# Softmax row sums counted by fours: every second pair sum is added to its neighbour by an accumulating DMA from GpSimd's queue

## Chip, cores and metric

One core of a Trainium2 chip. The metric is the device time of one execution in microseconds (us), the median over several runs; the comparison after the change is made in the same way.

## The reference

Input x is 16 samples of 192 channels by 32x32 positions (N = 1024 tokens), float32. The block is a group norm over 32 groups of 6 channels, six-head self-attention (head size 32), an output projection with a bias, and the residual.

```
...
        B, C, H, W = x.shape
        N = H * W
        xt = x.reshape(B, C, N).transpose(0, 2, 1)
        qkv = jnp.einsum('bnc,oc->bno', xt, qkv_w)
        qkv = qkv.reshape(B, N, 3, NUM_HEAD, DIM_HEAD).transpose(2, 0, 3, 1, 4)
        q, k, v = (qkv[0], qkv[1], qkv[2])
        attn = jnp.einsum('bhnd,bhmd->bhnm', q, k) * SCALE
        attn = jax.nn.softmax(attn, axis=-1)
        out = jnp.einsum('bhnm,bhmd->bhnd', attn, v)
        out = out.transpose(0, 2, 1, 3).reshape(B, N, C)
        out = jnp.einsum('bnc,oc->bno', out, proj_w) + proj_b
...
    x = x + _L0_conv_ref(_gn(x), L0_conv_qkv_w, L0_conv_proj_w, L0_conv_proj_b)
```

## The kernel before

The program is written as one instruction stream per engine, with semaphores between them. Work is cut into **steps**, one per sample (16 with attention, and a few at either end), and each step into 24 **slots**: three pairs of heads times eight tiles of 128 keys. In slot s TensorE makes the transposed scores of one key tile against all 1024 queries for the two heads of the pair, as four matmuls of 512 queries (units u = 0 to 3, `score`, L528). ScalarE turns each into exponentials `probs` (L681). TensorE then multiplies `probs` by V (`weigh`, L543), and needs their sum over the keys for the softmax's denominator.

**The denominator.** GpSimd adds the `probs` of slots s-1 and s elementwise (L751, two instructions, one for each head `a`), at the odd slots, into a ring of four `prob_pairs`. TensorE multiplies such a pair sum by a matrix of ones (`count`, L558), which adds up its 128 keys, and accumulates the four pairs of a head pair in the bank `sums_ps`. Then, once per head pair: ScalarE copies the sums (`copy_sums`, L656), SP spreads them over 128 partitions (L386), VectorE inverts them (L887), SP gathers and broadcasts them through DRAM (L393, L396), GpSimd divides the heads by them (L725), ScalarE and GpSimd split the result in two float16 parts (L624, L730), and SP moves these to the projection's operands (L411).

**Around it, in the same slots.** `row_max` (L453) makes the scores of twelve slots ahead for VectorE's row maxima (L825). `fill` (L511 to L516) makes, at fixed slots, one piece of the next sample's Q, K and V or of the last sample's projection. ScalarE and VectorE split the new Q and K in two float16 parts, `qk_hi` (L601) and `qk_lo` (L868), in one buffer. The last of the six pieces is made at slot 6; then, from slot 7 on, SP copies them within on-chip memory to the stacked operands `q_stack` and `k_stack` (`stack_pair`, L358), six DMAs of 128 KB for each head pair, at slots 7, 9 and 11. At slot 10 SP also loads the next x, 1 MB in three DMAs (L344, L346). At slot 13 ScalarE takes the first Q and K piece of the sample after the next into the same `qk_hi`, and so waits first until all 18 copies have landed:

```
                    if i == 0 and due(st.b + 2):

                        for p in range(PAIRS):
                            act.wait_ge(stacked[p], MOVE * STACK_MOVES * (st.b + 2))
```

ScalarE's queue is in order: the exponentials of slot 13 stand behind this wait, and TensorE has two score banks. What stands in which slot is given by tables (`QK_LATE_SLOTS`, `STACK_SLOTS`, `LOAD_SLOT`, `SUMS_TAKEN` and its neighbours), and `due(s, offset, every)` says which unit of work is due `offset` slots after it began. GpSimd issues no DMA in this kernel.

Of the kernel before, what the change touches and what calls it, by code (L numbers as in the profile page):

```python
# [16 lines left out]
C = 192  # L17
# [61 lines left out]
PAIR = 2  # L79
PAIR_COUNTED = PAIR + 3  # L80
PAIRS_A_HEAD = TILES // PAIR

HEADS_TAKEN = TILES
SUMS_TAKEN = TILES + 4
SUMS_SPREAD = TILES + 5
INVERTED = TILES + 6
INV_SPREAD = TILES + 7
DIVIDED = TILES + 11
MOVED = (23, 22, 22)
# [108 lines left out]
def group_norm_attention(nc, x, qkv_wT, proj_wT, proj_b, group_mean, identity, out):  # L198


    with ExitStack() as ctx:
        def sb(name, shape, dt):
            return ctx.enter_context(nc.sbuf_tensor(name, shape, dt))
# [18 lines left out]
        probs = sb("probs", [P, 2, RING, N], F32)  # L222
        prob_pairs = sb("prob_pairs", [P, 2, PAIR_RING, N], F32)

# [24 lines left out]

        w_f32 = prob_pairs[:, 0, 0:2, 0:3 * C]  # L250
        wp_f32 = prob_pairs[:, 0, 2:4, 0:C]
        w_abs = prob_pairs[:, 1, 0:2, 0:3 * C]
        wp_abs = prob_pairs[:, 1, 2:4, 0:C]
        w_hi = sb("w_hi", [P, 2, 3 * C], F16)
# [175 lines left out]
        def _(pe):  # L430
# [118 lines left out]
            def count(b, q):  # L549

                p, at_pair = divmod(q, PAIRS_A_HEAD)
                pe.wait_ge(pairs_added, 2 * (SLOTS // PAIR * b + q + 1))
                if at_pair == 0 and due(PAIRS * b + p):
                    pe.wait_ge(sums_taken, PAIRS * b + p)
                for half in range(HALVES):
                    for a in range(2):
                        at = D * (2 * half + a)
                        last = pe.matmul(sums_ps[at:at + D, :], ones[:, 0:D],  # L558
                                         prob_pairs[:, a, q % PAIR_RING, HALF * half:HALF * (half + 1)],
                                         start=(at_pair == 0), stop=(at_pair == PAIRS_A_HEAD - 1))  # L560
                last.then_inc(sums_done, 1)
# [5 lines left out]
            def step(st):  # L567
                for s in range(SLOTS):
                    for u in range(SCORE_UNITS):
# [18 lines left out]
        def _(act):  # L588
# [60 lines left out]
            def copy_sums(st, s):  # L649

                for j, par, p in st.due(s, SUMS_TAKEN, TILES):
                    k = PAIRS * j + p
                    act.wait_ge(sums_done, PAIRS_A_HEAD * (k + 1))
                    if due(k):
                        act.wait_ge(sums_spread_out, MOVE * k)
                    nc.scalar.copy(sums_sb[:, :], sums_ps[:, :]).then_inc(sums_taken, 1)  # L656
# [35 lines left out]
        def _(pool):  # L692
            nc.gpsimd.memset(k_stack[STACK:SHIFTED, :, :, :], SHIFT).then_inc(shift_set, 1)

            def step(st):
                for s in range(SLOTS):
                    if st.project_in and s == VAR_SLOT:

# [43 lines left out]
                    if st.attend and s % 2 == 1:  # L742

                        j = s // 2
                        for a in range(2):
                            pool.wait_ge(probs_ready, SCORE_UNITS * (SLOTS * st.b + s) + 2 * (a + 1))
                            counted = SLOTS // PAIR * st.b + j - PAIR_RING + 1
                            if a == 0 and due(counted):

                                pool.wait_ge(sums_done, counted)  # L750
                            nc.gpsimd.tensor_tensor(prob_pairs[:, a, j % PAIR_RING, :],  # L751
                                                    probs[:, a, (s - 1) % RING, :],
# [178 lines left out]
```

## Time and profile before

| | |
|---|---|
| median of 3 runs | 1878.63 us (1876.38 to 1881.58) |
| the profiled execution | 1886.8 us, span 1885.0 us |
| TensorE's mean granted clock | 0.96 |
| busy, TensorE / VectorE / ScalarE / GpSimd | 92% / 61% / 67% / 63% |
| moved by DMA | 109.28 MB, mean 58 GB/s |

The span is the time from the first to the last instruction; the profiled execution's own time is 1.8 us more. Busy shares are means over the whole span, and a matmul's row overlaps the next one's, so how much an instruction costs TensorE is read from the starts of the rows around it. The DMA share is the mean busy share of the core's 16 DMA engines.

### The profile page before, as it was taken

To read this page: it belongs to the slowest core of one execution; us is meant where nothing else is said; L and a number is where in the kernel's file an instruction comes from. 1 tells how busy PE (TensorE), PEld (TensorE's weight loads), DVE (VectorE), ACT (ScalarE), POOL (GpSimd) and SP (SyncE) were. 2 spreads that over 40 slices of the span, in tenths; PEclk is the share of its full clock that TensorE was granted. 3 is DMA by queue.
4 is the path that set the end of the run, shared out by engine and by line. 5 is a ranking of instruction groups with operands and counts; after the bars stand their busy time and mean duration, and the time that the engine had idled before them with its cause. 6 is when DMAs were issued, how large, how long until landed. Compare 5 with 4: busy or idle time off the path is not lost.

```text
span 1885.0 us, 30321 instructions
## 1 busy us (share of the span) xinstructions
PE 1727.9 (92%) x9440; PEld 531.2 (28%) x9440; DVE 1156.5 (61%) x2022; ACT 1257.5 (67%) x2033; POOL 1182.0 (63%) x613
## 2 busy tenths in 40 slices
PE   3799999999998999999999999999989999999993
PEld 1233223323232232322323222332223223222220
DVE  2577767666666666656666656766656666666710
ACT  1247777866677676766868667786666768777781
POOL 3126767755676666666766666675567666767783
PEclk9989999998999999999999999999999999999995
DMA  2404141402414033151402314141151404132102
GB/s 67 73 1 79 30 89 41 91 20 58 86 46 85 27 74 56 48 94 49 80 18 75 67 47 85 41 88 26 53 91 46 85 20 90 23 78 43 58 19 73
DMA packets 74285, 109.28 MB, mean 58 GB/s; under 512 B 26176, under 2 KB 39040, under 8 KB 74112
## 3 DMA queue, kind: packets, MB, share of 16 engines
q1 hardware_dynamic: 74112, 107.13, 26.8%
q8 instruction: 89, 1.46, 0.3%
q14 instruction: 84, 0.69, 0.1%
HBM read 42.99 MB, written 12.98 MB: 30 GB/s over the span
## 4 chain that ended last, share of the span: by engine, by line
PE 71%; DMA 10%; SPq 8%; ACT 4%; issue 4%; DVE 2%; POOL 1%; ACTq 0%; POOLq 0%; DVEq 0%
PE max_ps L453 17%; PE heads_ps L543 16%; PE scores_ps L528 15%; PE sums_ps L558 9%; DMA k_stack<-qk_lo 8%; SPq L358 6%; ACT probs L681 3%; PE extra_ps L516 2%; PE extra_ps L511 2%; PE extra_ps L512 2%; PE extra_ps L513 2%; PE extra_ps L515 2%; DMA inv_rows<-inv_spread 1%; PE extra_ps L475 1%; PE extra_ps L474 1%
## 5 line engine op out<-in xcount | busy, mean ns | idle before, releaser
L825 DVE TENSOR_REDUCE half_max<-max_ps 128x1 f32<-128x512 f32 x1536 | 1012.1, 685 | 524.7 <-PE max_ps L453 489.2
L681 ACT ACTIVATE probs<-scores_ps,exp_scale 128x512 f32<-128x512 f32 x1536 | 995.4, 686 | 442.0 <-PE scores_ps L528 416.7
L751 POOL TENSOR_TENSOR prob_pairs<-probs 128x1024 f32<-128x1024 f32 x384 | 898.2, 2357 | 482.2 <-ACT probs L681 480.0
L528 PE MATMUL scores_ps<-q_stack,k_stack 98*128 98x512 f16 x1536 | 598.5, 391 | 77.5 <-ACT probs L681 61.4
L453 PE MATMUL max_ps<-k_stack,q_stack 96*128 96x512 f16 x1536 | 608.1, 398 | 4.2 <-DMA k_stack<-qk_lo 2.2
L543 PE MATMUL heads_ps<-probs,v_sb 128*32 128x512 f32 x3072 | 416.4, 615 | 0.0
L453 PEld LDWEIGHTS max_ps<-k_stack,q_stack 96*128 96x128 f16 x1536 | 150.5, 98 | 615.6 <-issue 514.9
L558 PE MATMUL sums_ps<-prob_pairs,ones 128*32 128x512 f32 x1536 | 215.3, 634 | 1.7 <-POOL prob_pairs L751 1.7
L528 PEld LDWEIGHTS scores_ps<-q_stack,k_stack 98*128 98x128 f16 x1536 | 151.8, 99 | 219.4 <-ACT probs L681 132.3
L740 POOL TENSOR_TENSOR x_res<-projected,x_res 96x512 f32<-96x512 f32 x64 | 81.1, 1267 | 82.3 <-ACT projected L613 82.3
L868 DVE TENSOR_TENSOR qk_lo<-extra_ps,qk_hi 128x512 f16<-128x512 f32 x96 | 66.0, 688 | 86.9 <-ACT qk_hi L601 84.7
L601 ACT CAST qk_hi<-extra_ps 128x512 f16<-128x512 f32 x96 | 55.8, 581 | 91.2 <-DMA k_stack<-qk_lo 53.7
L543 PEld LDWEIGHTS heads_ps<-probs,v_sb 128*32 128x32 f32 x3072 | 61.1, 109 | 157.4 <-issue 147.1
L636 ACT ACTIVATE xhat<-x_sb,neg_mu_rstd,rstd 128x512 f32<-128x512 f32 x64 | 51.2, 806 | 40.1 <-POOL neg_mu_rstd L703 40.1
L725 POOL TENSOR_TENSOR heads_out<-heads_sb,inv_sb 128x512 f32<-128x512 f32 x48 | 60.7, 1265 | 17.1 <-DMA inv_sb<-inv_rows 15.1
L700 POOL TENSOR_TENSOR rstd<-var_eps,minus_half 128x2 f32<-128x2 f32 x16 | 11.2, 701 | 92.1 <-DVE var_eps L862 92.1
L730 POOL TENSOR_TENSOR heads_lo<-heads_out,heads_hi 128x512 f16<-128x512 f32 x48 | 55.4, 1154 | 14.0 <-ACT heads_hi L624 14.0
L613 ACT ACTIVATE projected<-extra_ps,bias,proj_unscale 96x512 f32<-96x512 f32 x64 | 49.4, 772 | 15.6 <-PE extra_ps L516 15.6
L511 PE MATMUL extra_ps<-xhat_a_hi,w_hi 128*128 128x512 f16 x96 | 38.5, 401 | 17.2 <-POOL xhat_b L716 9.4
L558 PEld LDWEIGHTS sums_ps<-prob_pairs,ones 128*32 128x32 f32 x1536 | 30.8, 109 | 68.4 <-issue 61.5
L511 PE MATMUL extra_ps<-attn_a_hi,wp_hi 128*96 128x512 f16 x64 | 25.4, 397 | 23.7 <-DMA attn_b<-heads_lo 21.1
L802 DVE BATCH_NORM_STATS2 half_stats<-x_sb 128x6 f32<-128x512 f32 x64 | 43.2, 682 | 0.0
(92 smaller groups left out, 1018.4 us busy)
## 6 DMA issues: line engine op xcount, KB each, us to landing
q_stack<-qk_hi SPq DMA_DIRECT2D x96, 128.0 KB, 4.4
k_stack<-qk_hi SPq DMA_DIRECT2D x96, 128.0 KB, 5.6
inv_sb<-inv_rows SPq DMA_DIRECT2D x48, 256.0 KB
x_res<-x SPq DMA_DIRECT2D x16, 768.0 KB, 5.4
out<-x_res SPq DMA_DIRECT2D x16, 768.0 KB, 4.8
x_sb<-x SPq DMA_DIRECT2D x16, 512.0 KB, 7.3
x_sb<-x SPq DMA_DIRECT2D x32, 256.0 KB, 8.7
q_stack<-qk_lo SPq DMA_DIRECT2D x48, 128.0 KB, 4.2
```

What stands on the lines that cost most here:

```text
L358: sp.dma_start(stack[D * n:D * (n + 1), par, 2 * p:2 * p + 2, :], part[row % P:row % P + 2 * D, row // P, :]).then_inc(stacked[p], MOVE)
L453: pe.matmul(max_ps[:, bank, :], q_stack[0:STACK, par, h, P * tile:P * (tile + 1)], k_stack[0:STACK, par, h, HALF * half:HALF * (half + 1)] ...
L511: pe.matmul(to, hi[:, 0, :], a_hi, start=True, stop=False)
L528: pe.matmul(scores_ps[:, u_bank(s, u), :], k_stack[0:SHIFTED, st.parity, h, P * tile:P * (tile + 1)], q_stack[0:SHIFTED, st.parity, h, HAL ...
L543: last = pe.matmul(heads_ps[at:at + D, :], v_sb[:, par, tile, D * h:D * (h + 1)], probs[:, a, s % RING, HALF * half:HALF * (half + 1)], st ...
L558: last = pe.matmul(sums_ps[at:at + D, :], ones[:, 0:D], prob_pairs[:, a, q % PAIR_RING, HALF * half:HALF * (half + 1)], start=(at_pair == ...
L681: nc.scalar.activation(probs[:, a, s % RING, HALF * half:HALF * (half + 1)], scores_ps[:, u_bank(s, u), :], ACT.Exp, scale=exp_scale[:, 0: ...
L725: nc.gpsimd.tensor_tensor(heads_out[:, :], heads_sb[:, (par + p) % 2, :], inv_sb[:, :], ALU.mult).then_inc(divided, 1)
L740: nc.gpsimd.tensor_tensor(x_res[:, t, n], projected[:, i % 2, :], x_res[:, t, n], ALU.add).then_inc(residual_added, 1)
L751: nc.gpsimd.tensor_tensor(prob_pairs[:, a, j % PAIR_RING, :], probs[:, a, (s - 1) % RING, :], probs[:, a, s % RING, :], ALU.add).then_inc( ...
L825: nc.vector.tensor_reduce(half_max[:, a, tile, half:half + 1], max_ps[:, bank, :], AX_X, ALU.max).then_inc(max_read[bank], 1)
L868: nc.vector.tensor_tensor(qk_lo[:, t, n], extra_ps[:, :], qk_hi[:, t, n], ALU.subtract).then_inc(extra_freed, 1)
```

## The change

GpSimd's pair sums stay. When both pairs of a quad (four slots) are there, GpSimd issues a DMA with an adding operation, from `prob_pairs` of the even pair onto that of the odd pair: 128 partitions of 8 KB, both heads at once, for which the tensor's axes are swapped so that the two heads of a ring place lie side by side. TensorE counts only the summed place, once in four slots instead of twice. The wait of `count` is on the DMA's semaphore. The count of a quad is due eight slots after its first tile (a pair's was five), so the sums, their inverse and the division each come one slot later; `MOVED`, the slots of L411, stays. In a ring place's reuse, the even one waits for the DMA that reads it, the odd one for the count. There are 96 such DMAs in all, six in a step.

```
@@ -77,15 +77,17 @@
 PAIR = 2
-PAIR_COUNTED = PAIR + 3
-PAIRS_A_HEAD = TILES // PAIR
+QUAD = 4
+QUAD_ADDED = QUAD
+QUAD_COUNTED = QUAD + 4
+QUADS_A_HEAD = TILES // QUAD
...
-SUMS_TAKEN = TILES + 4
...
-DIVIDED = TILES + 11
+SUMS_TAKEN = TILES + 5
...
+DIVIDED = TILES + 12
...
@@ -548,16 +552,16 @@
             def count(b, q):
 
-                p, at_pair = divmod(q, PAIRS_A_HEAD)
-                pe.wait_ge(pairs_added, 2 * (SLOTS // PAIR * b + q + 1))
+                p, at_quad = divmod(q, QUADS_A_HEAD)
+                pe.wait_ge(quad_summed[at_quad], MOVE * (PAIRS * b + p + 1))
...
-                                         prob_pairs[:, a, q % PAIR_RING, HALF * half:HALF * (half + 1)],
...
+                                         prob_pairs[:, (2 * q + 1) % PAIR_RING, a, HALF * half:HALF * (half + 1)],
...
@@ -692,8 +696,18 @@
+            def sum_quad(b, q):
+
+                pool.wait_ge(pairs_added, 4 * (SLOTS // QUAD * b + q + 1))
+                pool.sem_inc(quad_begun, 1)
+                pool.dma_start(prob_pairs[:, (2 * q + 1) % PAIR_RING, :, :].rearrange("p a n -> p (a n)"),
+                               prob_pairs[:, 2 * q % PAIR_RING, :, :].rearrange("p a n -> p (a n)"),
+                               accum_op=ALU.add).then_inc(quad_summed[q % QUADS_A_HEAD], MOVE)
+
             def step(st):
                 for s in range(SLOTS):
+                    for j, par, q in st.due(s, QUAD_ADDED, QUAD):
+                        sum_quad(j, q)
...
-                            counted = SLOTS // PAIR * st.b + j - PAIR_RING + 1
-                            if a == 0 and due(counted):
-
-                                pool.wait_ge(sums_done, counted)
-                            nc.gpsimd.tensor_tensor(prob_pairs[:, a, j % PAIR_RING, :],
+                            q, second = divmod(j - PAIR_RING, 2)
+                            if a == 0 and second == 0 and due(PAIRS * st.b + q // 2 + 1):
+
+                                pool.wait_ge(quad_summed[q % 2], MOVE * (PAIRS * st.b + q // 2 + 1))
+                            elif a == 0 and second == 1 and due(SLOTS // QUAD * st.b + q + 1):
+
+                                pool.wait_ge(sums_done, SLOTS // QUAD * st.b + q + 1)
+                            nc.gpsimd.tensor_tensor(prob_pairs[:, j % PAIR_RING, a, :],
                                                     probs[:, a, (s - 1) % RING, :],
                                                     probs[:, a, s % RING, :], ALU.add).then_inc(pairs_added, 1)
```

Where the instructions stand now. GpSimd's queue, slots 7 to 11 of a step in the loop (the first L751 row is the second half of slot 7's pair, the next two are slot 9's pair, L707 and L716 make low parts of the normalised x; register rows are left out), before:

```order
L751 TENSOR_TENSOR prob_pairs<-probs 128x1024 [waits probs_ready]
...
L707 TENSOR_TENSOR xhat_a_lo<-xhat,xhat_a_hi 128x1024 [waits xhat_ready]
...
L751 TENSOR_TENSOR prob_pairs<-probs 128x1024 [waits sums_done]
...
L751 TENSOR_TENSOR prob_pairs<-probs 128x1024 [waits probs_ready]
...
L716 TENSOR_TENSOR xhat_b<-xhat,xhat_b 64x1024 [waits pairs_added]
...
L725 TENSOR_TENSOR heads_out<-heads_sb,inv_sb 128x512 [waits heads_lo_ready,inv_broadcast]
```

and with the change (line numbers are those of the changed file: L768 is the pair sum, L703 the adding DMA):

```order
L768 TENSOR_TENSOR prob_pairs<-probs 128x1024 [waits probs_ready]
...
L703 DMA prob_pairs<-prob_pairs 128x2048 [waits pairs_added]
...
L721 TENSOR_TENSOR xhat_a_lo<-xhat,xhat_a_hi 128x1024 [waits xhat_ready]
...
L768 TENSOR_TENSOR prob_pairs<-probs 128x1024 [waits quad_summed0]
...
L768 TENSOR_TENSOR prob_pairs<-probs 128x1024 [waits probs_ready]
...
L730 TENSOR_TENSOR xhat_b<-xhat,xhat_b 64x1024 [waits pairs_added]
...
L768 TENSOR_TENSOR prob_pairs<-probs 128x1024 [waits sums_done,probs_ready]
...
L768 TENSOR_TENSOR prob_pairs<-probs 128x1024 [waits probs_ready]
...
L703 DMA prob_pairs<-prob_pairs 128x2048 [waits pairs_added]
...
L739 TENSOR_TENSOR heads_out<-heads_sb,inv_sb 128x512 [waits heads_lo_ready,inv_broadcast]
```

Two adding DMAs, of the quads of slots 4 to 7 and 8 to 11, now stand behind the pairs of slots 7 and 11, and the division has moved behind the second of them.

SP's queue, slots 5 to 7 of a step (L380 are shift rows for the scores, L411 the moved heads, L358 the first stack), before:

```order
L386 DMA sums_spread<-sums_sb 128x1x16 [waits sums_taken]
L380 DMA q_stack<-shift_rows 1x16x128 [waits shift_step]
L380 DMA q_stack<-shift_rows 1x16x128
L411 DMA attn_a_hi<-heads_hi 64x512 [waits heads_lo_ready]
L411 DMA attn_a_lo<-heads_lo 64x512
L411 DMA attn_a_hi<-heads_hi 64x512
L411 DMA attn_a_lo<-heads_lo 64x512
L358 DMA q_stack<-qk_hi 32x2x1024 [waits extra_freed]
L358 DMA q_stack<-qk_lo 32x2x1024
```

and now:

```order
L384 DMA q_stack<-shift_rows 1x16x128 [waits shift_step]
L384 DMA q_stack<-shift_rows 1x16x128
L390 DMA sums_spread<-sums_sb 128x1x16 [waits sums_taken]
L415 DMA attn_a_hi<-heads_hi 64x512 [waits heads_lo_ready]
L415 DMA attn_a_lo<-heads_lo 64x512
L415 DMA attn_a_hi<-heads_hi 64x512
L415 DMA attn_a_lo<-heads_lo 64x512
L362 DMA q_stack<-qk_hi 32x2x1024 [waits extra_freed]
L362 DMA q_stack<-qk_lo 32x2x1024
```

The spreading of the sums has moved behind the shift rows; the order of L411 and L358 (now L415, L362) is the same, but the `heads_lo` that L415 waits for is made one slot later on GpSimd.

TensorE's queue at an odd slot with a count before (L558, here followed by a row maximum and a score):

```order
L516 MATMUL extra_ps<-xhat_b,w_lo 128x512
L552 ISA
L558 MATMUL sums_ps<-prob_pairs,ones 32x512 [waits pairs_added]
L558 MATMUL sums_ps<-prob_pairs,ones 32x512 x3
L453 MATMUL max_ps<-k_stack,q_stack 128x512 [waits max_read1]
L527 ISA
L528 MATMUL scores_ps<-q_stack,k_stack 128x512 [waits probs_ready]
```

and at one of the slots, a multiple of four, where a count stands now (L562):

```order
L519 MATMUL extra_ps<-xhat_b,w_hi 128x512
L520 MATMUL extra_ps<-xhat_b,w_lo 128x512
L562 MATMUL sums_ps<-prob_pairs,ones 32x512 [waits quad_summed1]
L562 MATMUL sums_ps<-prob_pairs,ones 32x512 x3
L457 MATMUL max_ps<-k_stack,q_stack 128x512 [waits max_read1]
L532 MATMUL scores_ps<-q_stack,k_stack 128x512 [waits probs_ready]
```

The group is the same four matmuls; its wait has gone from GpSimd's pair to the DMA's semaphore, and there are half as many groups.

## Rows read from the trace of the kernel before

**Rows 1.** The page's head: busy us, share of the span, instructions.

```profile
PE 1727.9 (92%) x9440; PEld 531.2 (28%) x9440; DVE 1156.5 (61%) x2022; ACT 1257.5 (67%) x2033; POOL 1182.0 (63%) x613
```

**Rows 2.** The page's chain that ended last, share of the span by engine.

```profile
PE 71%; DMA 10%; SPq 8%; ACT 4%; issue 4%; DVE 2%; POOL 1%; ACTq 0%; POOLq 0%; DVEq 0%
```

**Rows 3.** The page's group of the counting matmuls, eight instructions for each count.

```profile
L558 PE MATMUL sums_ps<-prob_pairs,ones 128*32 128x512 f32 x1536 | 215.3, 634 | 1.7 <-POOL prob_pairs L751 1.7
```

**Rows 4.** Timeline around a count: start, duration (us), engine, line, tiles.

```profile
910.72 0.38 PE L453 MATMUL max_ps<-k_stack,q_stack 96*128 96x512 f16 x1
...
910.94 0.38 PE L528 MATMUL scores_ps<-q_stack,k_stack 98*128 98x512 f16 x1
...
911.25 1.06 PE L558 MATMUL sums_ps<-prob_pairs,ones 128*32 128x512 f32 x8
...
912.24 0.39 PE L453 MATMUL max_ps<-k_stack,q_stack 96*128 96x512 f16 x1
```

**Rows 5.** What L601 waits for (us, times); first and last such wait in the timeline.

```profile
  DMA k_stack<-qk_lo: 53.7, 12
...
272.97 0.58 ACT L601 CAST qk_hi<-extra_ps 128x512 f16<-128x512 f32 x1 [3.53 <-DMA k_stack<-qk_lo]
...
1504.21 0.58 ACT L601 CAST qk_hi<-extra_ps 128x512 f16<-128x512 f32 x1 [4.54 <-DMA k_stack<-qk_lo]
```

**Rows 6.** Timeline at one of these waits (idle before it in brackets).

```profile
831.77 0.58 ACT L601 CAST qk_hi<-extra_ps 128x512 f16<-128x512 f32 x1 [4.72 <-DMA k_stack<-qk_lo]
...
834.61 1.93 PE L558 MATMUL sums_ps<-prob_pairs,ones 128*32 128x512 f32 x8
```

**Rows 7.** SP's queue in that step: moved heads, first copies, last copy, store.

```profile
799.44 0.59 SPq L411 DMA_DIRECT2D attn_a_hi<-heads_hi  x1
...
802.88 0.60 SPq L358 DMA_DIRECT2D q_stack<-qk_hi  x1
...
810.65 0.56 SPq L358 DMA_DIRECT2D q_stack<-qk_hi  x1
...
819.73 0.60 SPq L358 DMA_DIRECT2D k_stack<-qk_lo  x1
...
882.53 0.52 SPq L423 DMA_DIRECT2D out<-x_res  x1
```

**Rows 8.** Stretches: five engines' busy us, granted clock, DMA share, GB/s.

```profile
808.00:811.00 3.00, 3.00 (x22) 1.47 (x24) 2.09 (x4) 2.60 (x5) 2.13 (x2) 1.00 0.14 25
...
811.00:814.00 3.00, 3.00 (x21) 0.58 (x14) 1.87 (x3) 2.99 (x6) 2.06 (x1) 1.00 0.74 152
814.00:820.00 6.00, 5.88 (x35) 1.67 (x33) 4.27 (x7) 4.44 (x8) 5.61 (x4) 1.00 1.07 163
...
826.00:829.00 3.00, 2.68 (x15) 0.65 (x14) 1.05 (x2) 1.05 (x2) 0.16 (x1) 1.00 0.78 103
...
883.00:886.00 3.00, 1.69 (x11) 0.35 (x10) 0.05 (x1) 0.90 (x2) 0.31 (x1) 1.00 0.91 281
```

**Rows 9.** The same stretch of two steps, with and without a load of x.

```profile
811.00:828.00 17.00, 16.88 (x103) 4.73 (x95) 10.66 (x17) 12.51 (x21) 13.84 (x7) 1.00 1.00 158
...
1596.00:1613.00 17.00, 16.88 (x99) 5.01 (x98) 11.43 (x19) 12.57 (x21) 13.99 (x8) 1.00 0.57 86
```

**Rows 10.** GpSimd's timeline in that step.

```profile
791.16 1.16 POOL L730 TENSOR_TENSOR heads_lo<-heads_out,heads_hi 128x512 f16<-128x512 f32 x1
795.04 4.67 POOL L751 TENSOR_TENSOR prob_pairs<-probs 128x1024 f32<-128x1024 f32 x2 [2.72 <-ACT probs L681]
803.37 4.67 POOL L751 TENSOR_TENSOR prob_pairs<-probs 128x1024 f32<-128x1024 f32 x2 [3.65 <-ACT probs L681]
...
820.37 4.68 POOL L751 TENSOR_TENSOR prob_pairs<-probs 128x1024 f32<-128x1024 f32 x2
```

**Rows 11.** The last count and what TensorE waits for behind it.

```profile
1843.25 1.06 PE L558 MATMUL sums_ps<-prob_pairs,ones 128*32 128x512 f32 x8 [1.66 <-POOL prob_pairs L751]
...
1865.41 0.63 PE L511 MATMUL extra_ps<-attn_a_hi,wp_hi 128*96 128x512 f16 x1 [21.10 <-DMA attn_b<-heads_lo]
```

More of the change, by code:

```diff
@@ L79 @@
 PAIR = 2
-PAIR_COUNTED = PAIR + 3
-PAIRS_A_HEAD = TILES // PAIR
+QUAD = 4
+QUAD_ADDED = QUAD
+QUAD_COUNTED = QUAD + 4
+QUADS_A_HEAD = TILES // QUAD
 HEADS_TAKEN = TILES
-SUMS_TAKEN = TILES + 4
-SUMS_SPREAD = TILES + 5
-INVERTED = TILES + 6
-INV_SPREAD = TILES + 7
-DIVIDED = TILES + 11
+SUMS_TAKEN = TILES + 5
+SUMS_SPREAD = TILES + 6
+INVERTED = TILES + 7
+INV_SPREAD = TILES + 8
+DIVIDED = TILES + 12
 MOVED = (23, 22, 22)
@@ L222, in group_norm_attention @@
         probs = sb("probs", [P, 2, RING, N], F32)
-        prob_pairs = sb("prob_pairs", [P, 2, PAIR_RING, N], F32)
+        prob_pairs = sb("prob_pairs", [P, PAIR_RING, 2, N], F32)
         xhat_a_hi = sb("xhat_a_hi", [P, 2, N], F16)
@@ L247, in group_norm_attention @@
         projected = sb("projected", [OM, 2, HALF], F32)
[L250 to L253, printed above, removed]
+        w_f32 = prob_pairs[:, 0:2, 0, 0:3 * C]
+        wp_f32 = prob_pairs[:, 2:4, 0, 0:C]
+        w_abs = prob_pairs[:, 0:2, 1, 0:3 * C]
+        wp_abs = prob_pairs[:, 2:4, 1, 0:C]
         w_hi = sb("w_hi", [P, 2, 3 * C], F16)
@@ L305, in group_norm_attention @@
         pairs_added = sem("pairs_added")
+        quad_begun = sem("quad_begun")
+        quad_summed = [sem(f"quad_summed{i}") for i in range(QUADS_A_HEAD)]
         heads_done = sem("heads_done")
@@ L549, in count @@
             def count(b, q):
-                p, at_pair = divmod(q, PAIRS_A_HEAD)
-                pe.wait_ge(pairs_added, 2 * (SLOTS // PAIR * b + q + 1))
-                if at_pair == 0 and due(PAIRS * b + p):
+                p, at_quad = divmod(q, QUADS_A_HEAD)
+                pe.wait_ge(quad_summed[at_quad], MOVE * (PAIRS * b + p + 1))
+                if at_quad == 0 and due(PAIRS * b + p):
                     pe.wait_ge(sums_taken, PAIRS * b + p)
@@ L558, in count @@
                         last = pe.matmul(sums_ps[at:at + D, :], ones[:, 0:D],
-                                         prob_pairs[:, a, q % PAIR_RING, HALF * half:HALF * (half + 1)],
-                                         start=(at_pair == 0), stop=(at_pair == PAIRS_A_HEAD - 1))
+                                         prob_pairs[:, (2 * q + 1) % PAIR_RING, a, HALF * half:HALF * (half + 1)],
+                                         start=(at_quad == 0), stop=(at_quad == QUADS_A_HEAD - 1))
                 last.then_inc(sums_done, 1)
@@ L579, in step @@
                         if u == COUNT_UNIT:
-                            for j, par, q in st.due(s, PAIR_COUNTED, PAIR):
+                            for j, par, q in st.due(s, QUAD_COUNTED, QUAD):
                                 count(j, q)
@@ L652, in copy_sums @@
                     k = PAIRS * j + p
-                    act.wait_ge(sums_done, PAIRS_A_HEAD * (k + 1))
+                    act.wait_ge(sums_done, QUADS_A_HEAD * (k + 1))
                     if due(k):
```

## Prediction

> **What bounds the kernel now.** I read the page's head first: TensorE is busy 92% of the span, ScalarE 67%, GpSimd 63% [rows 1]. That looks as if TensorE work taken out came off the time one for one. The chain that ended last says otherwise: only 71% of the span lies on TensorE, 10% on DMA transfers and 8% on SP's queue [rows 2]. So a part of every step is bound by something that TensorE doesn't do. To find it I asked who ends ScalarE's idle time at L601: the copies to `k_stack`, 53.7 us in 12 waits, some 4.5 us each, one in each of 12 consecutive steps, from 272.97 to 1504.21 us, which is 11 periods of 111.9 us [rows 5]. In one of them, at 831.77 us, ScalarE has stood 4.72 us; the exponentials stand behind it, so TensorE stands too, and its next count takes 1.93 us, where one takes 1.06 elsewhere [rows 4, 6].
>
> Why are the copies late? SP begins them at 802.88 and issues the last at 819.73 [rows 7], and it lands only when ScalarE goes on, 12 us later. The DMA share is 0.14 at 808 to 811 us, 0.74 at 811 to 814, and 1.07 at 814 to 820 [rows 8]; over 811 to 828 us it is 1.00 [rows 9]. The engines are full: copies and the load of x queue up behind each other. The step without a load of x is a natural experiment. In the like stretch its share is 0.57, TensorE runs through (16.88 busy of 17), and it isn't among the 12 waits [rows 5, 9]. One plain transfer of 1 MB more or less in this window makes or unmakes the wait.
>
> So a step has two parts. From slot 7 (the last `qk_lo` piece) to slot 13 (ScalarE goes on) the length is set by SP's issues and the DMA engines, about 29 us (802.88 to 831.77). In the other 18 slots it is TensorE's order that sets it.
>
> **What is removed.** 96 of 192 counts. From a score to the next instruction TensorE needs 0.22 us; with a count between it is 1.30 (910.94 to 912.24) [rows 4]. So 1.08 us each, 104 us in all; the group's busy time, half of 215.3 us [rows 3], says the same. A step gives 6.5 us. But of its 12 counts three stand in slots 7 to 12, where the end is set by a landing, and what is saved there only makes ScalarE wait sooner. Outside stand nine, at odd slots; with the change four, at slots 16, 20, 0 and 4. That is 5 x 1.08 = 5.4 us a step that counts.
>
> **What is added.** Six adding DMAs a step, each 128 rows of 8 KB. The trace has no such DMA, nor any from GpSimd, so I bound it. Let E be the time for which one fills all 16 engines. The stretch with the 768 KB store of the output (issued 882.53) moves 281 GB/s at share 0.91 [rows 7, 8], so 309 GB/s at full share: 1.05 MB take 3.4 us. That is the low end, a copy in long rows beside little else. An adding DMA must read the destination as well as the source, so twice that, 6.8 us, is the value that I take. The load of x, also 1 MB, costs (1.00 - 0.57) x 17 = 7.3 us of engine time beside the copies [rows 9]. Reading twice at that price gives the high end, about 15.
>
> The Trainium skill, "Collectives: The Full Stack", section "The bandwidth ceiling: the fold count and why AG ≠ RS ≠ AR", says the same of reductions in a DMA engine: they are half as fast as copies because each chunk needs two source reads on one ring, not because the add costs time. By that rule E is twice the copy, whatever the copy costs. No run here shows it yet.
>
> **Where the six lie.** GpSimd issues a quad's DMA behind its second pair. Two matter. The pair of slot 7 ends at 803.37 + 4.67 = 808.04, that of slot 11 at 820.37 + 4.68 = 825.05 [rows 10]. The issue itself is unseen: between SP's 0.6 us [rows 7] and one pair sum's 2.3 us [rows 10]; I take 1.2. GpSimd is idle 37% of the span [rows 1] and waits for probs before each pair, which hides it. So the DMAs start near 809.3 and 826.3.
>
> The first meets 1.5 us of idle engines until 811 (0.86 of 1.7 us) and 0.8 until 814 (0.26 of 3); the rest, E - 2.3, pushes the whole backlog back. The second starts when, with that push, copies for several microseconds are still queued (826 to 829 shows 0.78 even before the change [rows 8]); nearly all of it goes before the last copy, E - 0.8. A third thing is late: `heads_lo` of the second head pair was ready at 791.16 + 1.16 and is now made behind the pair that ends at 795.04 + 4.67 = 799.7, so at 800.9. SP waits for it before the first copy: its four issues took from 799.44 to about 802, and now go from 800.9 to 803.5, so the copies start 0.6 us later [rows 7, 10].
>
> The landing that ScalarE waits for moves by 0.6 + (E - 2.3) + (E - 0.8) = 2E - 2.5. With E = 6.8 that is 11.1 us, its wait grows to 16 to 18 us, and a step changes by 11.1 - 5.4 = +5.7. Twelve steps: +68 us.
>
> **The rest.** The first step and the last with a copy have spare share (0.57) and I set them at zero. Two more steps have no such copies and gain 6.5 each: -13. At the end, the last count stood right behind the last pair (1843.25), and 21 us later TensorE still waits for what follows from it [rows 11]; now the DMA stands between, 1.2 for the issue and 6.8 for the transfer: +8. The other quads find idle engines, and TensorE counts four slots (some 17 us) after their issue, so they cost nothing while E plus latency is under that; if this cover goes, TensorE and all behind it waits. The swapped axes cost nothing: the pair sum still reads and writes 1024 contiguous elements. The later inverse and division hide behind the same 24-slot order; what is late next is the SP issue counted above.
>
> Sum: 68 - 13 + 8 = +63 us, against the profiled execution 1886.8 to 1950. That execution is 8 us above the median, so I give 1878.6 + 63 = **1942 us**. In general: 1878.6 + 12 (2E - 7.9) - 5.
>
> **Rivals.**
> - *The adding DMA is cheap* (E near 3.4: the reads overlap). A step changes by -1.1, the total is 1860. It turns at 2E - 7.9 = 0.4, so E = 4.15 us. For it: 309 GB/s is what these engines reach in long rows [rows 8]. Against: the x load, in rows of 4 KB, cost 7.3 us in this very window. Chance 0.17.
> - *The copies aren't pushed* (the engines give SP's queue its turns, and the gain outside arrives in full): 1878.6 - 12 x 5.4 - 13 + 8 = 1809. Against it: the x load alone made the wait. Chance 0.07.
> - *The adding DMA is slow* (E of 10 to 15). At E = 12 the step grows by 16.1, 2067; at 15 it is 2139. Then the first quad, beside the copies, also comes too late for the count of slot 12, which adds TensorE's wait to ScalarE's. For it: copies here run at 163 GB/s at share 1.07, half of the store's rate [rows 8]. Chance 0.16.
> - *Forecast*, E between 5 and 9: 1900 to 1996. Chance 0.60.
>
> In sentences of their own: the Trainium skill, "DMA: Bandwidth & Descriptors", section "Anatomy of one DMA — SWDGE (gpsimd) path", gives a fit, 2.0 us fixed plus bytes over 436 GB/s. By it, as an estimate, 1 MB fills the engines 2.4 us, and the total would be about 1836, by the first rival's mechanism. The trace's copies (163 GB/s) disagree with the rate, the store (281) comes closer; for an adding DMA no row here decides.
>
> **How the numbers follow.** 1942 is the likeliest case's value at E = 6.8. The range must leave out at most 2 in 10: 1855 takes in nearly all of the cheap case, 2067 the slow one up to E = 12. About 0.3% (6 us) is what a measurement of this kernel can tell from none. Faster by more: the cheap case but a slice near its turn, and the unpushed case, 0.22. Within: that slice, 0.05. Slower: 0.73.
>
> **What would show each step.** In the changed profile: the counting group at x768 and half the busy time; L605 (L601 now) waiting for `k_stack` 12 or more times with 12 to 20 us each, where it was 4.5; a period of about 118 us; the DMA share at 1.0 from some 809 us of the step's like place through the wait, and in the 20-to-4 slots between 0.2 and 0.5; the adding DMA's 16 engines filled for 6.8 us. Wrong: an E under 4.15, waits at L605 that stay under 10 us, or waits of TensorE at L562 for the DMA of 5 us and more in each step, which would say that the DMA's own latency, not its share of the engines, decides.

## The result, and the profile after

The changed kernel takes 1954.45 us (median of 4 runs, 1949.09 to 1960.23), the kernel before, run beside it, 1877.51 (1872.37 to 1881.58). The ratio is 1.0406, with a 95% interval of 1.0378 to 1.0434: slower by 77 us. The forecast was 1942.

The page of the changed kernel's profile (line 1: busy time and share of each engine; the queue lines: packets, MB, share of the 16 engines over the span; then the chain that ended last, then groups of instructions, then a DMA group):

```profile
span 1958.4 us, 28917 instructions
PE 1666.9 (85%) x8672; PEld 523.6 (27%) x8672; DVE 1154.4 (59%) x2022; ACT 1245.4 (64%) x2033; POOL 1270.0 (65%) x709
...
q0 software_dynamic: 13824, 100.67, 26.2%
q1 hardware_dynamic: 74112, 107.13, 25.2%
...
PE 45%; DMA 15%; SPq 13%; POOL 12%; issue 7%; ACT 4%; DVE 2%; POOLq 0%; ACTq 0%; DVEq 0%
...
L605 ACT CAST qk_hi<-extra_ps 128x512 f16<-128x512 f32 x96 | 56.5, 589 | 226.7 <-DMA k_stack<-qk_lo 189.2
...
L703 POOL DMA_DIRECT2D prob_pairs<-prob_pairs x96 | 84.7, 882 | 56.9 <-POOL prob_pairs L768 55.5
L562 PE MATMUL sums_ps<-prob_pairs,ones 128*32 128x512 f32 x768 | 106.6, 628 | 11.3 <-DMA prob_pairs<-prob_pairs 11.3
...
prob_pairs<-prob_pairs POOLq DMA_DIRECT2D x96, 1024.0 KB, 8.5
```

The counting group is half of what it was [rows 3]. The chain on TensorE went from 71% [rows 2] to 45%. ScalarE's wait for `k_stack` took 53.7 us [rows 5] and takes 189.2. GpSimd's queue q0 is the adding DMAs alone: 26.2% of 1958.4 us over 96 is **E = 5.34 us** each, and one lands 8.5 us after its issue (median). The DMA is almost never waited for by its own reader: TensorE lost 11.3 us to it in all, at one place, the last count.

One step, that of [rows 6 to 10]. First ScalarE, on the timeline (start, duration, in brackets the idle time before it and what ended it):

```profile
864.93 0.59 ACT L605 CAST qk_hi<-extra_ps 128x512 f16<-128x512 f32 x1 [15.15 <-DMA k_stack<-qk_lo]
```

then SP's queue:

```profile
828.20 0.60 SPq L362 DMA_DIRECT2D q_stack<-qk_hi  x1
...
836.34 1.28 SPq L362 DMA_DIRECT2D q_stack<-qk_hi  x1
837.66 1.39 SPq L362 DMA_DIRECT2D q_stack<-qk_lo  x1
...
844.18 0.61 SPq L362 DMA_DIRECT2D q_stack<-qk_hi  x1
...
847.41 0.59 SPq L362 DMA_DIRECT2D k_stack<-qk_lo  x1
```

GpSimd's two issues in the window:

```profile
828.36 4.67 POOL L768 TENSOR_TENSOR prob_pairs<-probs 128x1024 f32<-128x1024 f32 x2 [2.73 <-ACT probs L685]
833.61 0.87 POOL L703 DMA_DIRECT2D prob_pairs<-prob_pairs  x1 [0.59 <-POOL prob_pairs L768]
...
849.18 0.88 POOL L703 DMA_DIRECT2D prob_pairs<-prob_pairs  x1 [0.58 <-POOL prob_pairs L768]
```

and stretches of the same step (length, busy us of PE, PEld, DVE, ACT, POOL with counts, granted clock, DMA share, GB/s):

```profile
828.00:834.00 6.00, 6.00 (x43) 2.67 (x45) 4.49 (x8) 5.53 (x11) 5.06 (x3) 1.00 0.62 143
834.00:842.00 8.00, 7.75 (x44) 1.81 (x36) 5.35 (x9) 6.84 (x13) 7.76 (x5) 1.00 0.95 186
842.00:850.00 8.00, 8.00 (x52) 2.76 (x52) 5.25 (x9) 5.46 (x9) 7.18 (x5) 1.00 1.06 175
850.00:859.00 9.00, 2.88 (x21) 0.56 (x13) 0.69 (x1) 0.00 (x0) 1.36 (x2) 0.80 1.09 193
859.00:865.00 6.00, 0.00 (x0) 0.00 (x0) 0.00 (x0) 0.07 (x1) 0.00 (x0) 0.50 0.33 78
865.00:872.00 7.00, 5.84 (x18) 1.49 (x19) 4.43 (x9) 5.18 (x9) 5.23 (x3) 0.50 0.01 1
872.00:880.00 8.00, 7.87 (x45) 2.70 (x44) 6.13 (x11) 5.52 (x10) 4.52 (x3) 0.97 0.15 36
```

Read together: the first adding DMA is issued at 833.61, and the share goes to 0.95 and stays near or over 1.0 until 859. From 850 to 859 TensorE is busy only 2.88 us, and from 859 until ScalarE goes on nothing computes. The copies' first issue to ScalarE's going on takes 828.20 to 864.93, 36.7 us, where it was 28.9 [rows 6, 7]. SP's own issues, 0.60 us each before, take up to 1.39 in the microseconds behind the first adding DMA's issue; at 844.18, with the share at 1.06, they take 0.61 again. TensorE's granted clock falls to 0.50 (the lower level, 1.2 GHz) while it stands, stays there until 872 although it works again from 865 on, and is back at 0.97 in the stretch from 872.

Twelve waits of about 15 us (14.74 at 280.60, 15.18 at 1564.76) stand in the place of the twelve of 4.5; two shorter ones, 3.64 at 171.37 and 5.95 at 1670.38, are new. The period is (1564.76 - 280.60)/11 = 116.7 us, where it was 111.9 [rows 5].

The end of the program, on the timeline:

```profile
1914.67 1.94 PE L562 MATMUL sums_ps<-prob_pairs,ones 128*32 128x512 f32 x8 [11.28 <-DMA prob_pairs<-prob_pairs]
```

The last pair sum ended at 1901.03 + 4.91 = 1905.94 on GpSimd; the last count, once right behind it, now stands 8.7 us later.

**Where the 73.4 us of the span went** (1885.0 to 1958.4). Up to the first of the twelve waits +7.6 (272.97 to 280.60), in the eleven periods after it +52.9, from the last wait to the end of the last pair sum +2.2, and behind it +10.7.

### The profile page after: what moved, and what is told of

Same layout as the page of the kernel before. It is cut to its first block, busy times and chain, and to the rows that moved or that the text cites. A ratio compares the mean times of both kernels' runs of the same rounds, so it can differ in the third digit from the quotient of the medians.

```text
span 1958.4 us, 28917 instructions
## 1 busy us (share of the span) xinstructions
PE 1666.9 (85%) x8672; PEld 523.6 (27%) x8672; DVE 1154.4 (59%) x2022; ACT 1245.4 (64%) x2033; POOL 1270.0 (65%) x709
## 3 DMA queue, kind: packets, MB, share of 16 engines
q0 software_dynamic: 13824, 100.67, 26.2%
q1 hardware_dynamic: 74112, 107.13, 25.2%
## 4 chain that ended last, share of the span: by engine, by line
PE 45%; DMA 15%; SPq 13%; POOL 12%; issue 7%; ACT 4%; DVE 2%; POOLq 0%; ACTq 0%; DVEq 0%
DMA k_stack<-qk_lo 12%; PE max_ps L457 11%; PE scores_ps L532 11%; PE heads_ps L547 11%; SPq L362 10%; POOL prob_pairs L768 9%; ACT probs L685 3%; PE sums_ps L562 3%; DMA inv_rows<-inv_spread 2%; SPq L415 2%; PE extra_ps L520 2%; POOL heads_out L739 1%; PE extra_ps L515 1%; PE extra_ps L516 1%; PE extra_ps L519 1%
## 5 line engine op out<-in xcount | busy, mean ns | idle before, releaser
L768 POOL TENSOR_TENSOR prob_pairs<-probs 128x1024 f32<-128x1024 f32 x384 | 898.1, 2358 | 473.7 <-ACT probs L685 469.7
L532 PE MATMUL scores_ps<-q_stack,k_stack 98*128 98x512 f16 x1536 | 609.9, 398 | 200.3 <-ACT probs L685 169.2
L547 PE MATMUL heads_ps<-probs,v_sb 128*32 128x512 f32 x3072 | 423.9, 625 | 0.9 <-ACT probs L685 0.9
L605 ACT CAST qk_hi<-extra_ps 128x512 f16<-128x512 f32 x96 | 56.5, 589 | 226.7 <-DMA k_stack<-qk_lo 189.2
L703 POOL DMA_DIRECT2D prob_pairs<-prob_pairs x96 | 84.7, 882 | 56.9 <-POOL prob_pairs L768 55.5
L562 PE MATMUL sums_ps<-prob_pairs,ones 128*32 128x512 f32 x768 | 106.6, 628 | 11.3 <-DMA prob_pairs<-prob_pairs 11.3
L754 POOL TENSOR_TENSOR x_res<-projected,x_res 96x512 f32<-96x512 f32 x64 | 85.5, 1336 | 40.5 <-ACT projected L617 40.5
L739 POOL TENSOR_TENSOR heads_out<-heads_sb,inv_sb 128x512 f32<-128x512 f32 x48 | 74.9, 1560 | 20.4 <-DMA inv_sb<-inv_rows 20.4
L628 ACT CAST heads_hi<-heads_out 128x512 f16<-128x512 f32 x48 | 29.7, 619 | 29.3 <-POOL heads_out L739 29.3
L904 DVE RECIPROCAL inv_spread<-sums_spread 128x16 f32<-128x16 f32 x48 | 11.7, 244 | 61.8 <-DMA sums_spread<-sums_sb 61.8
## 6 DMA issues: line engine op xcount, KB each, us to landing
x_res<-x SPq DMA_DIRECT2D x16, 768.0 KB, 10.7
```

The source lines that it names most:

```text
L532: pe.matmul(scores_ps[:, u_bank(s, u), :], k_stack[0:SHIFTED, st.parity, h, P * tile:P * (tile + 1)], q_stack[0:SHIFTED, st.parity, h, HAL ...
L547: last = pe.matmul(heads_ps[at:at + D, :], v_sb[:, par, tile, D * h:D * (h + 1)], probs[:, a, s % RING, HALF * half:HALF * (half + 1)], st ...
L562: last = pe.matmul(sums_ps[at:at + D, :], ones[:, 0:D], prob_pairs[:, (2 * q + 1) % PAIR_RING, a, HALF * half:HALF * (half + 1)], start=(a ...
L703: pool.dma_start(prob_pairs[:, (2 * q + 1) % PAIR_RING, :, :].rearrange("p a n -> p (a n)"), prob_pairs[:, 2 * q % PAIR_RING, :, :].rearra ...
L739: nc.gpsimd.tensor_tensor(heads_out[:, :], heads_sb[:, (par + p) % 2, :], inv_sb[:, :], ALU.mult).then_inc(divided, 1)
L754: nc.gpsimd.tensor_tensor(x_res[:, t, n], projected[:, i % 2, :], x_res[:, t, n], ALU.add).then_inc(residual_added, 1)
```

## The experiments

Ratios are to the kernel before, run beside each on the same chip, with the 95% interval. Three numbers of a step tell most of each run, read from the timelines as means over the same eleven steps in every run (those of the second to the last of the twelve waits, each with a load of x): W, from SP's first stack copy to ScalarE's going on; R, the rest of the step; and their sum, the period. Before: W 28.7, R 83.5, period 112.3. After: 36.6, 80.5, 117.1.

**1. The adding DMAs cut to 16 elements** (`e1_tiny`).

```diff
-                pool.dma_start(prob_pairs[:, (2 * q + 1) % PAIR_RING, :, :].rearrange("p a n -> p (a n)"),
-                               prob_pairs[:, 2 * q % PAIR_RING, :, :].rearrange("p a n -> p (a n)"),
+                pool.dma_start(prob_pairs[:, (2 * q + 1) % PAIR_RING, 0, 0:16],
+                               prob_pairs[:, 2 * q % PAIR_RING, 0, 0:16],
```

> The changed kernel with each of the 96 adding DMAs cut to 16 elements in each partition (8 KB becomes 64 B), everything else as it is; the sums are then not the full ones, so only its time is read. Theory (the DMAs' share of the 16 engines in the window of slots 7 to 13 is what costs): ScalarE's waits for the copies fall from 15 to about 5 or 6 us, the period of a step from 116.7 to about 107, the time to 1800 to 1830 us, which is also what halving the counts is worth by itself. Rival (what costs is all that comes with them: GpSimd's issue of 0.88 us, the wait for a semaphore of a DMA, sums that are a slot later): the time stays above 1900.

1841.58 us, 0.981 (0.977 to 0.985). W 28.4, R 80.8. The time lies 12 us above the theory's range, and far below the rival's. The transfers are worth 1954 - 1842 = 113 us, so it is their bytes, not their issues or the new waits, that make the kernel slower. But the gain that is left, 38 us, is half of what the removed counts were to bring. A second cost or a smaller gain stood open.

**2. Only the two quads inside the window cut** (`e2_window`): those issued at slots 8 and 12, the other four whole.

```diff
+                if q % 6 in (1, 2):
+                    pool.dma_start(prob_pairs[:, (2 * q + 1) % PAIR_RING, 0, 0:16],
+                                   prob_pairs[:, 2 * q % PAIR_RING, 0, 0:16],
+                                   accum_op=ALU.add).then_inc(quad_summed[q % QUADS_A_HEAD], MOVE)
+                else:
```

> Only the two adding DMAs that are issued at slots 8 and 12 of a step are cut to 16 elements; the other four of a step stay whole (the sums are incomplete, only its time is read). Theory (only the two in the window cost): within 20 us of the run with all six cut, so 1805 to 1850. Rival (each of the six costs alike, a third of the loss each pair): two thirds of the difference remain, about 1905.

1845.67, 0.983 (0.979 to 0.986); W 28.3. That is 4 us from run 1 and inside its interval, while q0 still fills the engines 19.0% of the span. Four of six adding DMAs a step cost nothing that can be measured; the other two cost all of it.

**3. Plain copies in the place of the adding ones** (`e3_copy`).

```diff
-                               prob_pairs[:, 2 * q % PAIR_RING, :, :].rearrange("p a n -> p (a n)"),
-                               accum_op=ALU.add).then_inc(quad_summed[q % QUADS_A_HEAD], MOVE)
+                               prob_pairs[:, 2 * q % PAIR_RING, :, :].rearrange("p a n -> p (a n)")).then_inc(quad_summed[q % QUADS_A_HEAD], MOVE)
```

> The same DMAs from the same queue as plain copies, without the adding operation (the sum of the even pair is lost, only its time is read). Theory (an adding DMA reads twice, a copy once): the share of queue q0 falls from 26.2% to between 13 and 17%, E from 5.3 to about 3 us, ScalarE's waits from 15 to about 10 us, the time to 1890 to 1915. Rival (the rows or the writes cost, the second read doesn't): share, waits and time as with the adding DMA, about 1954.

1898.61, 1.010 (1.007 to 1.014). Its page:

```profile
span 1904.0 us, 28917 instructions
...
q0 software_dynamic: 13824, 100.67, 15.3%
...
L605 ACT CAST qk_hi<-extra_ps 128x512 f16<-128x512 f32 x96 | 56.5, 589 | 178.9 <-DMA k_stack<-qk_lo 142.8
...
prob_pairs<-prob_pairs POOLq DMA_DIRECT2D x96, 1024.0 KB, 4.9
```

A copy of the same bytes fills the engines 0.153 x 1904.0 / 96 = 3.03 us and lands in 4.9; the addition makes that 5.34 and 8.5, 1.76 times. The window grows with E: 2E - 2.5 is 3.6 for the copy and 8.2 for the addition; W grew by 4.5 and by 7.8, so by 1.4 us for each us of E rather than 2.

The Trainium skill, "Collectives: The Full Stack", section "The bandwidth ceiling: the fold count and why AG ≠ RS ≠ AR", puts a reduction at twice a copy, since it reads two sources. The measured 1.76 is near that rule and below it.

**4. The load of x two slots later, in the changed kernel** (`e4_load12`).

```diff
-LOAD_SLOT = 10
+LOAD_SLOT = 12
```

> The changed kernel whole, with the load of the next x issued behind the last copies (slot 12 instead of 10) in SP's queue. Theory (all bytes ahead of the last copy count, whoever moves them): the load's 5 to 7 us of engine time leave the way, ScalarE's waits fall from 15 to 8 to 10 us in 12 steps, the time to 1870 to 1900. Rival (the copies' own rate, from 64-partition rows of 2 KB, sets the landing, and the load fits between them): waits of 14 us and more, 1940 to 1955.

1853.59, 0.990 (0.983 to 0.997), so 101 us below the changed kernel, more than expected. W 29.0, R 78.9. SP's queue is in order: the 1 MB load stood ahead of the last six copies and now stands behind them. The waits for `k_stack` fall to 7.4 us each, 95.6 us in 13. The 15 us waits need both the adding DMAs and the load in the window. What the adding DMAs still cost without the load is seen against run 6.

**5. The kernel before with every second count left out, no DMA** (`e5_half_counts`).

```diff
+                if at_pair % 2 == 0:
+                    pe.sem_inc(sums_done, 1)
+                    return
...
-                                         start=(at_pair == 0), stop=(at_pair == PAIRS_A_HEAD - 1))
+                                         start=(at_pair == 1), stop=(at_pair == PAIRS_A_HEAD - 1))
```

> The kernel before with only every second pair sum counted (the other is left out, so the denominators are too small and only the time is read); no DMA from GpSimd, nothing moved. It shows what the removed TensorE work is worth by itself. Theory A (outside the window TensorE sets the pace, as the prediction has it): -5.4 us in 12 steps and -6.5 in two, 1795 to 1810. Theory B (once TensorE is lighter, GpSimd's pair sums and what hangs on them set the pace in part of the slots, as the run with tiny DMAs suggests by its 1842): 1825 to 1845.

1820.33, 0.969 (0.966 to 0.972). W 28.1, R 79.7, period 107.8. The time lies between the ranges of the two theories and decides for neither. The removed counts alone give 59 us, not the 78 of the forecast (12 x 5.4 + 13). In the loop they give 4.5 a step. Since run 1 has the same counts and stands at 1842, another 21 us lie in the rest of the change.

**6. The load two slots later in the kernel before** (`e6_before_load12`), the same edit as in run 4.

> The kernel before, with the load of the next x issued at slot 12 instead of 10. Theory (the same queue of bytes sets ScalarE's wait there): the 12 waits of 4.5 us vanish, and with them some of the time at the lower clock, 1800 to 1825. Rival (the wait of the kernel before has another cause): 1870 to 1885.

1824.71, 0.972 (0.969 to 0.975); the waits for `k_stack` fall from 53.7 us [rows 5] to 11.3 in 9, W to 25.2 and the period to 106.8. One number in a table is worth 54 us in the kernel before: most of its wait was the load standing ahead of six copies. The waits fell by 42 us; the clock has a part in the rest. From just before the first of the twelve waits to 20 us behind the last, TensorE was busy 85.9 us at the lower level in the kernel before and 34.7 here, and work takes about twice as long there (a count 1.93 us against 1.06 [rows 4, 6]); so, as an estimate from these rows, up to 26 of the 54 us are the clock's.

Run 4 is this kernel with the change, and it takes 1853.59 against 1824.71. So with the load out of the way too, the change as written costs 29 us: W is 3.8 longer (29.0 for 25.2), and behind the last pair sum the program takes 53.1 us for 41.6.

**7. Quads only outside the window** (`e7_hybrid`): the two quads of slots 4 to 11 are counted as pairs again, without a DMA, and the others stay, so the sums are whole.

```diff
+COUNTED_APART = (1, 2)
...
+                if apart:
+                    pe.wait_ge(pairs_added, 4 * (SLOTS // QUAD * b + q + 1))
+                else:
+                    pe.wait_ge(quad_summed[at_quad], MOVE * (2 * b + MOVED_BEFORE[q]))
...
+                if q % 6 in COUNTED_APART:
+                    return
```

> The changed kernel, whole sums, but the two quads of a step whose adding DMA falls in the window (issued at slots 8 and 12) have no DMA: TensorE counts both of their pairs, one group of eight matmuls instead of four. Theory (their transfers cost, and TensorE's two more counts are hidden in ScalarE's wait): as the run with those two cut, 1840 to 1855. Rival (the extra counts lie on the path): 1860 to 1875.

1851.2, 0.987 (0.983 to 0.990); W 28.1, R 81.5. As in run 2, with true sums: the change done where the engines are idle is 1.3% faster than before.

**8. Run 7 with the load at slot 12 and the moved heads a slot later** (`e8_hybrid_lm`).

```diff
-LOAD_SLOT = 10
+LOAD_SLOT = 12
...
-MOVED = (23, 22, 22)
+MOVED = (23, 23, 22)
```

> The same with the load of x at slot 12 and the second head pair's moves to the projection behind the first six copies instead of ahead of them (MOVED 23, 23, 22). Theory: what is left of the waits, 6.5 us in 12 steps, goes with the load, 1770 to 1790. Rival (with the wait gone GpSimd's work, or the extra counts, set the pace): 1800 to 1830.

1825.45, 0.971 (0.967 to 0.975): no better than run 6, and not the 1770 to 1790 of the theory. W 26.3, R 81.1. With both repairs of the DMA side, something still ate what the counts gave. The second edit has a price of its own: the four moved heads, 2.6 us of SP's issues, now stand between the copies, and from SP's first copy to its last it takes 16.7 us where run 12, without that edit, has 14.7.

**9. Run 5 with GpSimd's issues** (`e9_half_issue`): 96 adding DMAs of 16 elements on a tensor of their own, no slot moved.

```diff
+                    for j, par, q in st.due(s, 4, 4):
...
+                        pool.dma_start(aside[:, 0:16], aside[:, 16:32],
+                                       accum_op=ALU.add).then_inc(aside_done, MOVE)
```

> The kernel before with half the counts left out, as in the run before that did so (1820), and six DMAs of 64 B a partition a step from GpSimd's queue at the slots where the changed kernel issues its own, on a tensor of their own; nothing is a slot later. The sums are too small, only the time is read. The run with tiny DMAs in the changed kernel took 1842, 21 us more than half counts alone. Theory A (GpSimd's issue, 0.88 us and the wait ahead of it, 96 times, delays its pair sums): 1835 to 1845. Theory B (the sums, and so the division and heads_lo ahead of the copies, are a slot later): 1815 to 1826.

1818.8, 0.967 (0.962 to 0.971), against 1820.33 without the issues.

```profile
L710 POOL DMA_DIRECT2D aside<-aside x96 | 84.5, 880 | 63.5 <-POOL prob_pairs L766 62.1
```

Each row is 0.88 us as in the changed kernel, and GpSimd hides all of them. So the 21 us between here and run 1 don't come from issuing. What else run 1 has is the slot by which sums, inverse and division come later, and with it counts that stand in slots 0, 4, 8 and so on, behind a DMA's semaphore, in place of the odd slots. From the last pair sum's start to the end it takes 53.7 us where runs 5 and 9 take 46.6 and 47.7, and its period is 109.2 us where theirs is 107.8 and 107.9. Its chain that ended last (start, duration, what) runs through the late division:

```profile
873.37 4.71 POOL prob_pairs L768 x2
...
879.27 1.59 POOL heads_out L739
...
884.79 2.37 POOL prob_pairs L768
887.15 1.12 POOL heads_lo L744
...
888.29 0.52 SPq L415
...
890.87 0.60 SPq L362
```

`heads_lo` is made behind a pair sum, SP waits for it at L415, and the first stack copy stands behind that. In run 9 SP's first copy goes when `qk_lo` is there, and POOL has 2% of the chain, in run 1 13%. But the chain says only what came last, not by how much: in run 1 the first copy is issued 0.37 us behind the last `qk_lo`, in run 9 0.06. This path carries 0.3 of the 1.3 us by which the periods differ. What carries the other 1.0 isn't shown; no run moves the counts' slots alone.

**10 and 11. VectorE adds the quads** (`e10_vector`), with the tables one slot earlier; and the same with the load at slot 12 (`e11_vector_load12`).

```diff
+            def sum_quad(b, q, a):
+
+                dve.wait_ge(pairs_added, 4 * (SLOTS // QUAD * b + q + 1))
+                to = prob_pairs[:, (2 * q + 1) % PAIR_RING, a, :]
+                nc.vector.tensor_tensor(to, prob_pairs[:, 2 * q % PAIR_RING, a, :], to, ALU.add).then_inc(quads_added, 1)
```

> Whole sums by quads, with VectorE adding the even pair onto the odd one (two instructions of 128x1024 a quad, one slot after the pair) in place of the DMA; the counts of a quad are due seven slots after its first tile and everything behind is in the slots of the kernel before. Theory (without a transfer and without a late slot the gain of half the counts, 59 us, comes whole, and VectorE, busy 59%, hides 200 us of adds): 1820 to 1835. Rival (adds of two SBUF operands run into GpSimd's and hold up the row maxima that TensorE waits for): 1845 to 1880.

> The same with the load of x at slot 12. Theory: the gains add, since the wait for the copies that is left (4.7 us with half the counts) goes: 1765 to 1790. Rival (the copies, begun sooner against a faster TensorE, are still what is waited for, or VectorE sets the pace): 1800 to 1830.

2221.3, 1.181 (1.176 to 1.185), and 2221.09, 1.182 (1.178 to 1.186): a plain miss of both expectations and their rivals. Two groups of run 10's page:

```profile
L758 POOL TENSOR_TENSOR prob_pairs<-probs 128x1024 f32<-128x1024 f32 x384 | 983.5, 2572 | 627.4 <-ACT probs L684 625.3
...
L839 DVE TENSOR_TENSOR prob_pairs<-prob_pairs 128x1024 f32<-128x1024 f32 x192 | 451.3, 2352 | 23.0 <-POOL prob_pairs L758 23.0
```

and a line of its list of waits (us in total, times, longest):

```profile
PEld max_ps L456 <- DVE half_max L832: 299.5, 242, 3.3
```

One addition takes 2.35 us on VectorE, and TensorE waits for the row maxima behind it. GpSimd's sums, too, grew from 2.36 to 2.57. The timeline shows that the two hold each other up (start, duration; the first row is two additions while GpSimd does nothing, the second one addition with GpSimd's pair sums under all of it):

```profile
2170.18 2.28 DVE L839 TENSOR_TENSOR prob_pairs<-prob_pairs 128x1024 f32<-128x1024 f32 x2
...
1668.13 3.13 DVE L839 TENSOR_TENSOR prob_pairs<-prob_pairs 128x1024 f32<-128x1024 f32 x1
```

12 additions a step are 28 us; the load of x no longer matters. The DMA was the better carrier.

**12. Run 8 with the tables of the kernel before** (`e12_hybrid_early`): counts, sums, inverse, division and moved heads go back a slot, the sums are whole.

```diff
-QUAD_COUNTED = QUAD + 4
+QUAD_COUNTED = QUAD + 3
...
-SUMS_TAKEN = TILES + 5
...
-DIVIDED = TILES + 12
-MOVED = (23, 23, 22)
+SUMS_TAKEN = TILES + 4
...
+DIVIDED = TILES + 11
+MOVED = (23, 22, 22)
```

> Whole sums. The adding DMAs only outside the window (the quads of slots 8 and 12 counted as pairs), the load of x at slot 12, and the counts of a quad due seven slots after its first tile instead of eight, so that the sums, the inverse, the division and the moves stand again in the slots of the kernel before; it was 1825 with all that a slot later. Theory (the late slot delays heads_lo ahead of the copies and costs the 20 us that lie between half counts alone, 1820, and the changed kernel with tiny DMAs, 1842): 1795 to 1812, the best version, below both the kernel before and the kernel before with the load moved (1825). Rival (the lateness costs nothing here, or a DMA that takes 8.5 us to land now makes TensorE wait in each quad): 1820 to 1850.

**1777.65 us, 0.946 (0.943 to 0.949)**: 5.4% under the kernel before, 47 us under run 6 and 48 under run 8, and better than expected. W 25.3, R 78.3, period 103.6.

```profile
q0 software_dynamic: 9216, 67.11, 19.1%
...
PE 75%; DMA 7%; ACT 6%; SPq 5%; issue 4%; DVE 2%; POOL 2%; ACTq 0%; POOLq 0%; DVEq 0%
...
L614 ACT CAST qk_hi<-extra_ps 128x512 f16<-128x512 f32 x96 | 55.8, 582 | 47.7 <-PE extra_ps L522 37.2
...
prob_pairs<-prob_pairs POOLq DMA_DIRECT2D x64, 1024.0 KB, 7.5
```

Four adding DMAs a step move 67 MB in all, and the engines are full of them 19.1% of the span. Hardly a step waits: `k_stack` ends 10.4 us of ScalarE's idle time in 11 waits, where run 8 has 54.9 in 13, and most of its idle time at L614 is now ended by TensorE. TensorE was busy at the lower clock for 32.7 us in the loop here and for 86.3 in run 8, counted as in run 6. Between runs 8 and 12 two things change, the tables and the place of the moved heads, so the 48 us aren't one cause's.

## Why the prediction was right

The mechanism and the sign were right: adding DMAs push copies that ScalarE waits for, and that costs more than the counts give. That the size came out near as well, 1942 forecast and 1954 measured, is partly luck. Against the span the sum was +63 and the trace has +73.4, but several terms were off and partly cancel. With the measured E of 5.34 the prediction's own formula, 1878.6 + 12 (2E - 7.9) - 5, gives 1907, which is 47 us too low; an E taken too large made up for 35 of them.

- **Outside the window 5.4 us, inside nothing.** Right in kind: W fell by only 0.6 when counts were left out (run 5). R fell by 3.9 there, not 5.4: the term was 1.5 us too large. By the starts of the exponentials in run 5, a removed count shortened its slot and the next together by 0.7 to 1.0 us; why not by the 1.08 between its neighbours wasn't isolated.
- **The adding DMA reads twice, E = 6.8.** It is 5.34, between the value taken and the low end of 3.4, and 1.76 times a copy (run 3). The doubling was nearly right; the copy under it, 3.03, was overestimated by the store's 3.4.
- **The landing moves by 2E - 2.5.** Near at two values of E, though the slope is 1.4 rather than 2 (run 3). With E = 5.34 it gives 8.2 us and 7.8 were measured, where the forecast had 11.1. Only the two quads of the window matter (run 2), and most because the load of x is in the same place: without it they lengthen W by 3.8 us (run 4 against run 6).
- **The step.** Forecast 11.1 - 5.4 = +5.7, measured +7.8 in W and -3.1 in R, +4.8 in the period: both terms too large. The first of the waits and the periods give 7.6 + 52.9 = 60.5 for the forecast's 68.
- **The wait of 16 to 18 us** at L605 was about 15.
- **Steps without copies, -13.** This failed: from the last wait to the end of the last pair sum nothing was gained (+2.2). Part of that is the last step with copies, which still waits 5.95 us at 1670.38. Behind the last copy the changed kernel gained 2.6 us, runs 1 and 5 some 6 (137.3 us from its issue to the last pair before; 134.7, 130.7 and 131.5 in these).
- **The end, +8.** 8.7 us for the DMA, 10.7 with what follows.
- **The slot later hides.** This was called free but for 0.6 us, and it isn't. Copies began 0.4 us behind `qk_lo` in the changed kernel, near what was forecast for SP, but run 1 leaves 21 us against run 5. Some 7 of them lie behind the last pair sum, where the last count waits 3.0 us for its small DMA, and most of the others in the periods. `heads_lo` before the stack copies carries 0.3 us a step of it. The rest goes with the lateness, or with the slots in which the counts now stand; that wasn't taken apart. The 48 us between runs 8 and 12 hold the order of the moved heads and the clock as well.
- **The clock** has no term in the prediction. Here it is small: TensorE was busy at the lower level 95.7 us in the loop, counted as in run 6, for 85.9 before.

Of the rivals, the cheap DMA was to turn at E = 4.15. The plain copy of run 3 has 3.03, and by the formula a step would shorten by 1.8 us and the total be 1851; its period grew by 2.0, and it takes 1899. W is off by 0.9 of that, R, which fell by 2.5 and not 5.4, by 2.9: the same two terms, the count's worth and the lateness, put the turn lower than I had it. That copies aren't pushed is refuted by W, a slow DMA by E.

## What to carry to other kernels

The mean DMA share says nothing on whether a transfer is free: four adding DMAs of 1 MB a step cost nothing that could be measured, two in a stretch that was already full (share 1.00 over 17 us [rows 9]) cost over 100 us. Look for that stretch by the instruction that waits for a landing, and put bulk loads behind urgent copies in the same queue before adding to it. Putting a side chain off by one slot wasn't free here (21 us between runs 1 and 5, with the small DMAs' own landing in it, and most of it with an open cause); try the old table with the new work before taking the delay as given. And when a chain names a path, read from the timeline how far behind the next path stands: in run 1 it was 0.3 us.

## What was not expected of the hardware

- An adding DMA of 1 MB within on-chip memory, 128 rows of 8 KB, fills the 16 engines 5.34 us, the plain copy 3.03, and lands in 8.5 us against 4.9. Its issue is a row of 0.88 us on GpSimd, the copy's 0.59.
- Behind the first adding DMA's issue, within 6 us of it, three of SP's issues take 1.03 to 1.39 us in place of 0.60. Of the 288 stack copies' issues 51 take over 1 us, where the kernel before has 8 and the plain copies of run 3 have 22. Full engines alone don't do this: at share 1.07 in the kernel before [rows 8] and 1.06 in the changed one SP's rows are 0.60 and 0.61.
- An elementwise addition of 128x1024 float32 from on-chip memory takes VectorE 1.15 to 1.22 us while GpSimd does nothing (three rows of run 10) and 2.54 on average with GpSimd busy beside it for over nine tenths of the row (120 rows). GpSimd's own takes 2.35 alone and 2.80 beside one of these. The Trainium skill, "GPSIMD Engine Reference", section "1. Specifications", says that GpSimd's interface to that memory is shared with VectorE, with contention when VectorE has two inputs there; the rows of run 10 agree.
